# Written-out first projections with a narrow gate, and the first maxima of the modulated attention inside the last chunks

## The reference, cut to what matters

```python
q = (hidden_states @ Wq + bq)      # 16 heads of 16; k and v likewise
scores = einsum('bhqd,bhkd->bhqk', q, k) / sqrt(16)
mod = sigmoid(hidden_states @ cg_W + cg_b + (cons_vec @ am_W + am_b))   # one gate for each token and head
scores = scores * mod.transpose(0, 2, 1)[..., None]
ctx = einsum('bhqk,bhkd->bhqd', softmax(scores), v)
causal_ctx = _mha(hidden_states, hidden_states, ca_Win, ...)            # 4 heads of 64: its q2, k2, v2
```

## Time and profile before

| | |
|---|---|
| median of 3 runs | 3923.17 us (3921.38 to 3924.82) |
| time of the profiled execution | 3921.55 us |
| its span | 3919.9 us |
| PE, DVE, ACT, POOL busy in the span | 89%, 58%, 38%, 39% |
| projections, first to last matmul of a job | 9.97 to 203.90 us |
| first maximum's matmul, first scores | 211.24 us, 250.28 us |

### The profile page before, as it was taken

One profiled execution on the slowest core, in us unless ns is written; L12 is line 12 of the kernel. 1 busy time (PEld: TensorE's weight loads), 2 busy tenths in 40 slices (PEclk: granted clock), 3 DMA queues, 4 the chain that ended last, 5 costly groups with the idle time before them and its releaser, 6 DMA issues. The chain is left out here.

```text
span 3919.9 us, 55959 instructions
## 1 busy us (share of the span) xinstructions
PE 3506.6 (89%) x19432; PEld 1696.7 (43%) x19432; DVE 2286.6 (58%) x3885; ACT 1496.9 (38%) x2216; POOL 1525.7 (39%) x1311
## 2 busy tenths in 40 slices
PE   9989999997999889999879756687888989999995
PEld 4412222222333343333645455443664656556553
DVE  5679999995666317664632358977886631111112
ACT  2237777775444323444213244211662211111112
POOL 0142223222888505887336413053652322222221
PEclk9979999998999999999879865799999999999998
DMA  5622322321112151120522331354542113333333
GB/s 184 210 82 69 79 64 65 78 65 47 41 44 64 67 195 55 44 82 14 161 96 86 126 101 48 144 133 116 159 140 81 44 59 110 101 90 108 100 91 97
DMA packets 309776, 366.46 MB, mean 93 GB/s; under 512 B 54130, under 2 KB 241796, under 8 KB 308548
## 3 DMA queue, kind: packets, MB, share of 16 engines
q1 hardware_dynamic: 269972, 305.81, 25.0%
q0 software_dynamic: 30384, 50.90, 5.6%
q10 hardware_dynamic: 9216, 7.09, 0.6%
HBM read 228.00 MB, written 127.27 MB: 91 GB/s over the span
## 5 line engine op out<-in xcount | busy, mean ns | idle before, releaser
L626 DVE TENSOR_REDUCE modulated_mx<-modulated_ring 128x1 f32<-128x512 f32 x1024 | 657.2, 684 | 29.6 <-PE modulated_ring L533 23.6
L612 ACT ACTIVATE modulated_probs<-modulated_scores 128x1024 f32<-128x1024 f32 x512 | 496.1, 1021 | 142.7 <-PE modulated_scores L554 142.6
L3263 DVE TENSOR_TENSOR expert_h<-expert_gelu,expert_bank 128x512 f32<-128x512 f32 x128 | 88.1, 688 | 389.8 <-PE expert_bank L3192 389.8
L3234 ACT ACTIVATE expert_gelu<-expert_bank 128x512 f32<-128x512 f32 x128 | 76.4, 597 | 548.3 <-PE expert_bank L3192 548.3
L3152 POOL DMA_INDIRECT scratch_acc<-expert_y,expert_idx x64 | 100.8, 1574 | 429.7 <-DVE expert_y L3268 405.8
L1038 POOL TENSOR_TENSOR meta_total<-meta_total,meta_probs 128x1024 f32<-128x1024 f32 x96 | 227.3, 2368 | 58.5 <-ACT meta_probs L947 51.1
L1038 POOL TENSOR_TENSOR causal_total<-causal_total,causal_probs 128x1024 f32<-128x1024 f32 x96 | 227.5, 2369 | 54.7 <-ACT causal_probs L947 47.0
L969 DVE TENSOR_REDUCE meta_mx<-meta_maxima 128x2 f32<-128x1024 f32 x120 | 146.9, 1224 | 117.5 <-PE meta_maxima L834 117.0
L969 DVE TENSOR_REDUCE causal_mx<-causal_maxima 128x2 f32<-128x1024 f32 x120 | 146.9, 1224 | 115.9 <-PE causal_maxima L834 115.4
L947 ACT ACTIVATE meta_probs<-meta_scores 128x1024 f32<-128x1024 f32 x128 | 131.0, 1023 | 142.3 <-PE meta_scores L860 139.3
L947 ACT ACTIVATE causal_probs<-causal_scores 128x1024 f32<-128x1024 f32 x128 | 131.0, 1023 | 138.6 <-PE causal_scores L860 135.6
(11 more groups left out here) (547 smaller groups left out, 7403.4 us busy)
## 6 DMA issues: line engine op xcount, KB each, us to landing
scratch_v<-proj_v SPq DMA_DIRECT2D x8, 1024.0 KB, 6.8
ahead_ctx<-scratch_ctx SPq DMA_DIRECT2D x16, 512.0 KB, 4.6
scratch_M<-steps_snap SPq DMA_DIRECT2D x16, 512.0 KB, 3.3
chunk_raw_v<-scratch_v SPq DMA_DIRECT2D x64, 128.0 KB, 2.8
chunk_mem<-scratch_M SPq DMA_DIRECT2D x32, 256.0 KB, 3.1
first_wg<-x_WgT SPq DMA_DIRECT2D x8, 1024.0 KB, 5.0
first_wu<-x_WuT SPq DMA_DIRECT2D x8, 1024.0 KB, 7.0
first_wd<-x_WdT SPq DMA_DIRECT2D x8, 1024.0 KB, 6.7
```

Of the source, the lines that this page charges most:

```text
L612: nc.scalar.activation(probs[u % NPROBS][i][:], sc[i][:], ACT.Exp, scale=SCALE).then_inc(s_exp, 1)
L626: V.tensor_reduce(mx[h % 2][:, x // 2, 1 - j % 2, j // 2, x % 2:x % 2 + 1], ring[bank_of["max", 4 * m + j]][:], AX.X, ALU.max).then_inc(s_ ...
```

## The change

1. **The chunk loop is written out**, with plain counts on the semaphores.
2. **The gate is narrow.** Its 16 columns are repeated twice on the host (`cg_W2`, 32 columns), and one job of a chunk does it: PE takes four groups of 32 columns, each for 128 of the 512 tokens (8 matmuls of 128 columns, one PSUM bank). ACT takes one sigmoid of 128x128, and then issues 8 DMAs that lay each gate row 16 times into `mod`. The job for chunk c+1 stands in chunk c, after `k`; `mod` has two buffers.
3. **Main banks 4 instead of 7**; four others are the ring of the maxima.
4. **The split moves**: ACT makes the first bf16 part (a copy), DVE has 3 operations for each tile (subtract, cast, subtract with bf16 output).
5. **The first heads** are loaded by ACT at the start of chunk 3 (25 DMAs), not by POOL.
6. **Twelve units of maxima** are made in chunks 4 to 7, three a chunk: one after the first `k2` job, one after the second `v` job, one after the last (`later` in the diff). The shift of half 0 is made in chunk 6, turned in place of a gate job in chunk 7, and laid into q by POOL before the block ends. POOL fills the constant rows of slot 0 in chunk 0.
7. **`quad_attention`** starts with unit 0 at once. POOL's stream there is `place_shift(1)`, the fills of slots 1 and 2, then the loop over halves.

```diff
+        GROUPS, WIDE, QT = 4, P // 4, CH // 4
...
-        BANKS = 7
+        BANKS = 4
...
+        ring = [st.ps(f"ring{i}", [P, CH]) for i in range(Q)]
...
+        later = lambda c, x: [("max", 3 * (c - FIRST_MAX) + x, 0)] * (c >= FIRST_MAX)
+        jobs = [("gate", 0, 0)]
+        for c in range(NCH):
+            jobs += [(x, c, m) for x in PARTS for m in range(KD)] + [("gate", c + 1, 0) if c < LAST_CHUNK else ("turn", 0, 0)]
+            jobs += [("q2", c, 0), ("q2", c, 1), ("k2", c, 0)] + later(c, 0) + [("k2", c, 1), ("v", c, 0), ("v", c, 1)] + later(c, 1)
+            jobs += [("v", c, 2), ("v", c, 3)] + later(c, 2)
...
+
+            def make_gate(c):
+                job = ("gate", c, 0)
+                mm.wait(act, job)
+                if c:
+                    mod_laid.wait(act, c - 1)
+                act_s.done(nc.scalar.activation(gate[:], bank_of(job)[:, 0:QT], ACT.Sigmoid, bias=modb[:]), job)
+                act_s.wait(act, job)
+                if c >= 2:
+                    dve_s.wait(act, ("q", c - 2, KD - 1))
+                for r in range(GROUPS):
+                    for m in range(KD):
+                        at = r * WIDE + m * (P // HD16)
+                        mod_laid.done(act.dma_start(mod[c % 2][:, m, r * QT:(r + 1) * QT],
+                                                    gate[at:at + P // HD16, :].unsqueeze(1).broadcast_to([P // HD16, HD16, QT])))
...
+            for c in range(NCH):
+                if c == HEADS_AT:
+                    for x in (*PARTS, "v"):
+                        stored[x].wait(act, 1)
+                    load_heads(act, first["q"], scr["q_part"], QUERY_PARTS, 0, s_heads)
+                    load_heads(act, first["k"], scr["k_part"], KEY_PARTS, 0, s_heads)
+                    act.dma_start(first["v"][:].rearrange("p t j c -> p t (j c)"), scr["v1"][0:T, 0:P].rearrange("(t p) c -> p t c", p=P)).then_inc(s_heads, 16)
+                for m in range(KD):
+                    dve_s.wait(act, ("q", c, m))
+                    if c and m == 0:
+                        stored["q"].wait(act, c - 1)
...
+            def load(c):
+                if c >= 2:
+                    mm.wait(pool, ("v", c - 2, TT - 1))
+                loaded[c % 2].done(pool.dma_start(xT[c % 2][:], rows(io["hT"])[:, :, c * CH:(c + 1) * CH]))
+
+            load(0)
+            load(1)
+            fill_identity(nc, pool, ident[:], s_made)
+            pool.wait_ge(s_made, 2)
+            fill_shift_rows(nc, pool, first["k"], s_const)
+            for c in range(2, NCH):
+                load(c)
+            act_s.wait(pool, ("turn", 0, 0))
+            place_first = first["turned"][0]
+            for e, r in ((1, slice(32, 64)), (0, slice(96, 128))):
+                pool.dma_start(first["q"][r, 2 * e:2 * e + 2, 0:CH], place_first[r, :].unsqueeze(1).broadcast_to([32, 2, CH])).then_inc(s_placed, 16)
+            pool.wait_ge(s_placed, 32)
+
...
                     pool.dma_start(qs[s][r, 2 * e:2 * e + 2, cols], turned[h % 2][r, :].unsqueeze(1).broadcast_to([32, 2, CH])).then_inc(s_placed[h % 2], 16)
 
-            place_shift(0)
             place_shift(1)
+            pool.wait_ge(s_made, 1)
+            for s in range(1, SLOTS):
+                fill_shift_rows(nc, pool, ks[s], s_const[s])
             for h in range(HALVES):
```

More of the change, by code:

```diff
@@ L197, in fill_identity @@
                             pattern=[[-1, P]], channel_multiplier=1).then_inc(made, 1)
[L200 to L220 removed]
+MAX_AHEAD = 12
 def project_hidden(nc, io, scr):
@@ L316, in _ @@
-            with pe.Fori(0, NCH // 2) as i:
-                for n, job in enumerate(jobs):
-                    j, kind, m = job
-                    if m == 0 and kind == T_KINDS[0]:
-                        loaded[j].wait(pe, i)
-                    if (j, kind, m) in ((0, "q", 0), (0, "q2", 0)):
-                        have(pe, 1 if kind == "q" else 2)
-                    before, back = bank_before(jobs, BANKS, n)
-                    emptied(before).wait(pe, i, before, back)
-                    for kd in range(KD):
-                        if kind == "v":
-                            lhs, rhs = xT[j][:, kd, m * P:(m + 1) * P], wv[:, kd, :]
-                        else:
-                            lhs, rhs = w[kind][:, kd, m * P:(m + 1) * P], xT[j][:, kd, :]
-                        last = nc.tensor.matmul(bank[n % BANKS][:], lhs, rhs, start=(kd == 0), stop=(kd == KD - 1))
-                    mm.done(last, job)
+            nc.tensor.matmul(modps, am[:], cons[:], start=True, stop=False)
@@ new lines, in _ @@
+            for job in jobs:
+                kind, c, m = job
+                if kind == "max":
+                    maxima(c)
+                    continue
+                if kind == "gate":
+                    loaded[c % 2].wait(pe, c // 2)
+                if job in (("q", 0, 0), ("q2", 0, 0)):
+                    have(pe, 1 if kind == "q" else 2)
+                if place[job] >= BANKS:
+                    before = main[place[job] - BANKS]
+                    emptied[before[0]].wait(pe, before)
+                to = bank_of(job)
+                if kind == "turn":
+                    pe.wait_ge(s_shift, 1)
+                    pe.wait_ge(s_made, 2)
+                    for t in range(TT):
+                        last = nc.tensor.matmul(to[:, t * P:(t + 1) * P], first["shift"][0][:, t, :], ident[:], start=True, stop=True)
+                elif kind == "gate":
+                    for kd in range(KD):
+                        for r in range(GROUPS):
+                            last = nc.tensor.matmul(to[r * WIDE:(r + 1) * WIDE, 0:QT], wg[:, kd, :], xT[c % 2][:, kd, r * QT:(r + 1) * QT],
+                                                    start=(kd == 0), stop=(kd == KD - 1))
+                else:
+                    x = xT[c % 2]
+                    for kd in range(KD):
+                        lhs, rhs = (x[:, kd, m * P:(m + 1) * P], wv[:, kd, :]) if kind == "v" else (w[kind][:, kd, m * P:(m + 1) * P], x[:, kd, :])
+                        last = nc.tensor.matmul(to[:], lhs, rhs, start=(kd == 0), stop=(kd == KD - 1))
+                mm.done(last, job)
@@ L333, in _ @@
         @block.scalar
         def _(act):
-            act_s.start(act)
             have(act, 0)
```

372 lines of the change are left out of this document (184 added, 188 removed).

## The result

The changed kernel takes 3931.16 us (median of 16 runs, 3927.02 to 3935.27), the kernel before 3922.86 beside it (16 runs, 3917.76 to 3926.98): a ratio of 1.0019, 95% interval 1.0011 to 1.0026. The prediction was 3890 us, with a range up to 3904. The profiled execution took 3928.16 us, its span is 3926.4.

A forecast was written before the change was run, and what follows sets the result against it. PE was taken to bound the projections and DVE the unit loop. 38.1 us gained at the followed point, less 5.3 for DVE's wait and 1 for PE's clock, off 3921.55 gave 3889.7, rounded 3890; range 3876 to 3904.

The forecast's parts named there:

- What bounds the kernel: Whole kernel: PE bounds the projections, DVE the unit loop at about 2.6 us a unit.
- The gate on PE: Projections: the narrow gate job costs PE 0.8 us; a chunk takes 21.4 us, or 24.0 with maxima in chunks 4 to 6.
- ACT: Projections: ACT's chain between chunks, 16.8 us plus eight issues at 0.51, takes 20.9 us against PE's 21.4.
- rival (4): Projections: ACT's issues so dear that every chunk waits; no gain from 1.0 us an issue, 0.2% slower from 1.12; chance 0.05.
- Chunk 0: First projection chunk: first v starts at about 29 us, the chunk ends at 36.0, 0.5 later than before.
- Chunk 3: Projections: ACT's 25 head loads take 12.8 us at 0.51 each, of which 2.8 us are lost.
- The inputs: Projections: a gate needs its chunk's input a whole chunk earlier; 0 to 6 us over six gates, taken as 1.8.
- The boundary: Start of the block after the projections, at 207.7 us: PE stands 2.7 us for slot 1's load.
- POOL behind it: After the boundary: POOL's fills delay the sums, so DVE stands 5.3 us at its first reciprocal.
- The followed point: First maximum of head group 1 (unit 16's maxima, issued in unit 4): moves from 262.30 to 224.2 us, 38.1 earlier.
- (2): Projections: ACT's chain decides, with issues of 0.7 us; 3900 us (3896 to 3910), chance 0.18.
- (3): Projections: the maxima do not hide, and the reductions' 30.8 us appear instead of 10.3; 3910 us, chance 0.07.

The follow-up runs named there:

- pat_16x8: The changed kernel with each ACT gate move reading 16 gate-tile rows repeated 8 times, not 8 rows 16 times (right placing left out): 3915.1 us, one run.
- pat_plain: The changed kernel with each ACT gate move reading all 128 gate-tile rows one to one (right placing left out): 3899.0 us, one run.
- gate_sp: The changed kernel with the eight gate moves a chunk issued by SP and not by ACT: 3892.59 us, ratio 0.9923.

## Why the prediction was wrong, point by point

**What bounds the kernel: right.** PE bounds the projections, DVE the unit loop; from 300 us on the kernels run alike.

**The gate on PE: right, a little better.** 16 records of 128 columns in four groups take 0.64 us at the full clock (0.8 forecast). Where nothing holds PE up, chunks are 21.4 us without maxima and 23.6 with them (21.4 and 24.0 forecast).

**ACT: the step that failed.** "ACT's own issues come 0.51 us apart", from the earlier trace rows, so "20.9, against PE's 21.4", and "I take 0.51". The chain was right; the term was mis-sized. An issue cost 1.08 us, the chain became 16.8 + 8.6 = 25.4, and a chunk 26.7; the rest, 1.3 us, the sum did not have: behind each wait the v jobs run 1.8 us longer at the lower clock. The 0.51 came from ACT's eight loads of weights at the start, the 0.54 from two moves of POOL. Neither row is a move of this kind, in a row of eight, on ACT, beside stores. The prediction itself says that there is "no row of such an issue on ACT". A slack of 0.5 us a chunk cannot carry a term of 4.1 us that is known only from other kinds of move; the range, which ends at 3904, should have taken in what rival (4) names.

**Chunk 0: too short.** It was to end at 36.0 us; chunk 1's first q starts at 46.05. The first gate's eight moves took 6.68 us (4.1 forecast), the next eight 10.16, and the first v job waited 5.48 us, then ran at the lower clock. The landing was nearly right: DVE began with q at 21.48, 2.8 us after the last issue's end, where 2.5 were taken. The same step took 2.4 us in `pat_16x8` and 1.6 in `pat_plain`. So of the 1 to 2 us that the prediction would have added for moves on 8 DMA engines, 0.3 to 0.4 are seen.

**Chunk 3: right in kind, partly by luck.** 2.8 us were forecast for the head loads; in `gate_sp`, where ACT has only them, PE waits 2.7. But the 25 loads take 16.7 us of ACT in the changed kernel (91.18 to 107.87) and not 12.8, and the chunk is lengthened by more than its wait, as said under `gate_sp`.

**The inputs: right.** 1.8 us forecast, 1.2 measured, and 1.9 in `gate_sp`, where PE has no waits for ACT that give the loads more time.

**The boundary: right.** 2.7 us for slot 1's load, measured 2.45 (3.98 in `gate_sp`), released by `modulated_v` as said.

**POOL behind it: right in kind.** 5.3 us at the first reciprocal, measured 3.33, and in `gate_sp` 3.15. A relapse of PE's clock was put at 1 us: from slot 1's maximum to the reciprocal are 29.99 us before and 35.97 after, 5.98 in all, so 2.65 are left beside the wait, and the first eight value records there take 1.65 us instead of 1.07 (rows above and the earlier trace rows).

**The sum.** The followed point was to move by 38.1 us and moved by 0.2, 262.10 against 262.30. What is lost after it came on top as forecast in kind: 7.5 us up to the first `causal_maxima` matmul, where 6.3 were forecast. The time is 8.3 us longer.

**The rivals.** (4) was the case: the same chain with issues so dear that every chunk waits, "from 1.12 it is slower by 0.2%". All 64 moves average 1.11 (the rows of eight, 70.9 us, over 64), and the kernel is slower by 0.2%. So the formula priced the case that it gave 0.05, with some luck: its 72 issues were a rough count, the head loads cost 0.67 us each and not as much as a gate move, and the lower clock was not in it. The chance was wrong: it leaned on POOL's two moves. (2), the same cause at 0.7 us, is close to `pat_plain` at 0.75: the formula gives 3904 for 0.75, its range was 3896 to 3910, and one run took 3899.0. (3), maxima that don't hide, is refuted: they cost 3.4 to 6.0 us of projection time and bring 20.5 to 22.5.

## What to carry to other kernels

DMA issues on an engine that other engines wait for are work of that engine, and have to be costed from a row of the same kind of move on the same queue; if there is none, the range takes in twice the nearest price. Put them behind the instruction that releases others, or on a queue with nothing urgent behind them: here four issues a chunk moved past the copies of q2 and k2 were worth 29 us, and all eight moved to SP 39 us. When a term is uncertain by more than the slack it fills, the case in which it decides isn't a rival of 0.05.

## What the runs showed that I had not expected

The price of an issue is not a constant of its engine. The same 64 KB move took 1.08 to 1.12 us on ACT in five of the eight rows, 0.84 in the first and 1.27 in two, 0.84 on SP in a late chunk and 0.60 on POOL; on ACT 0.75 with 128 source rows and 0.97 with 16; mostly 0.61 for the first two of a row and up to 2.4 in its middle; 1.4 beside 25 head loads from another queue. That looks like an engine standing behind moves still in work, but no run separates this from other causes, and it stays open.

A wait of 3 us costs more than 3 us: PE came back at a lower granted clock (0.94 over the chunk against 1.00), and 16 records took 8.8 us instead of 7.03. In the changed kernel seven waits of 28.6 us go with four such v groups at +1.8 us each and more in the late chunks.

The Trainium skill ("DMA: Bandwidth & Descriptors", "Issuing engines are not separate DMA queues") says that starting DMAs from several engines saves only the sequencer's time, "which is usually small relative to the DMA itself". Here that time was 8.6 us a chunk on ACT, in front of the copy that PE waits for, and moving it to SP's stream made the difference between 3931 and 3893 us. What counts is what stands behind the issues, which the sentence leaves aside.
